# A transformer-like chain in float32 on one core: the shared expert's gate and up products made one product of 128 rows

## What is computed

```python
xn = layernorm(x)
x  = x + attn0(xn) + ffn0(xn)        # layer 0
xn = layernorm(x)
x  = x + attn1(xn) + ffn1(xn)        # layer 1

def ffn0(x):                         # 16 routed experts of 64, top 2, and one shared expert of 64
    shared = (silu(x @ ws_gate) * (x @ ws_up)) @ ws_down
    g = einsum('th,ehm->etm', x, w_gate)
    u = einsum('th,ehm->etm', x, w_up)
    eo = einsum('etm,emh->eth', silu(g) * u, w_down)
    return einsum('te,eth->th', route, eo) + shared
```

## Time and profile before

| what | value |
|---|---|
| median of 3 runs | 2215.48 us (2214.3 to 2218.01) |
| the profiled execution's own time | 2220.59 us |
| its span | 2218.7 us |
| PE busy in the span | 2071.2 us (93%) |
| DVE busy | 1567.6 us (71%) |
| ACT busy | 1207.9 us (54%) |
| POOL busy | 130.4 us (6%) |
| mean granted PE clock | 0.966 |

### The profile page before, as it was taken

One profiled execution on the slowest core, in us unless ns is written; L12 is line 12 of the kernel. 1 busy time (PEld: TensorE's weight loads), 2 busy tenths in 40 slices (PEclk: granted clock), 3 DMA queues, 4 the chain that ended last, 5 costly groups with the idle time before them and its releaser, 6 DMA issues.

```text
span 2218.7 us, 33619 instructions
## 1 busy us (share of the span) xinstructions
PE 2071.2 (93%) x12004; PEld 965.4 (44%) x12088; DVE 1567.6 (71%) x2854; ACT 1207.9 (54%) x2323; POOL 130.4 (6%) x251
## 2 busy tenths in 40 slices
PE   5958999989999999998999999999999999999889
PEld 3621233435656323343656523333565642334356
DVE  5667887756689788673769888775558978877154
ACT  1323677774341667776342367777534156777721
POOL 2000001100000001110000000110000000111000
PEclk9966999999999999999999999999999999999989
DMA  4060100100060010100015010010006001010000
GB/s 154 1 167 5 30 16 26 30 2 1 1 171 6 6 30 23 33 16 2 1 58 119 6 30 15 26 30 3 1 1 157 19 6 30 16 30 17 2 1 10
DMA packets 46983, 71.75 MB, mean 32 GB/s; under 512 B 7968, under 2 KB 17120, under 8 KB 46432
## 3 DMA queue, kind: packets, MB, share of 16 engines
q1 hardware_dynamic: 46816, 69.61, 11.9%
HBM read 46.25 MB, written 22.54 MB: 31 GB/s over the span
## 4 chain that ended last, share of the span: by engine, by line
PE 87%; DVE 5%; ACT 3%; issue 2%; DMA 1%; SPq 0%; POOL 0%; DVEq 0%; ACTq 0%
PE ps L1528 18%; PE ps L1503 16%; PE ps L1472 15%; PE ps L1376 8%; PE ps L1404 8%; PE ps L1396 8%; DVE row_max L1028 3%; PE ps L1538 2%; PE ps L1328 1%; ACT prob L1222 1%; PE ps L1316 1%; PE ps L1297 1%; PE ps L1505 1%; PE ps L1422 1%; PE ps L1322 1%
## 5 line engine op out<-in xcount | busy, mean ns | idle before, releaser
L1222 ACT ACTIVATE prob<-ps 128x512 f32<-128x512 f32 (+3 forms) x1792 | 864.2, 555 | 352.6 <-PE ps L1503 263.6
L1028 DVE TENSOR_REDUCE row_max<-ps 128x1 f32<-128x1024 f32 x512 | 606.1, 1219 | 112.4 <-PE ps L1472 111.7
L1503 PE MATMUL ps<-q_stack,k_stack 96*128 96x512 bf16 (+4 forms) x1760 | 542.6, 362 | 34.4 <-ACT prob L1222 18.7
L1472 PE MATMUL ps<-k_stack,q_stack 96*128 96x512 bf16 (+4 forms) x1740 | 516.6, 368 | 27.6 <-DVE row_max L1028 13.4
L1025 DVE CUSTOM_DVE_ANT_0 tmp<-ps,const_b 128x128 f32<-128x128 f32 (+7 forms) x512 | 371.6, 756 | 131.5 <-PE ps L1472 118.0
L1528 PE MATMUL ps<-prob,v_ones 128*32 128x512 f32 (+3 forms) x3584 | 438.2, 561 | 2.8 <-ACT prob L1222 2.3
L1503 PEld LDWEIGHTS ps<-q_stack,k_stack 96*128 96x128 bf16 (+1 forms) x1792 | 172.2, 98 | 353.6 <-ACT prob L1222 223.7
L1472 PEld LDWEIGHTS ps<-k_stack,q_stack 96*128 96x128 bf16 (+1 forms) x1792 | 149.8, 98 | 383.2 <-issue 100.5
L1376 PEld LDWEIGHTS ps<-wd,prob 128*128 128x128 f32 (+1 forms) x1600 | 206.9, 191 | 69.7 <-issue 62.7
L1165 ACT ACTIVATE prob<-ps 128x512 f32<-128x512 f32 x128 | 76.4, 597 | 272.4 <-PE ps L1396 272.3
L1376 PE MATMUL ps<-wd,prob 128*128 128x128 f32 (+1 forms) x1600 | 212.1, 276 | 1.3 <-DVE prob L933 1.3
(11 more groups left out here) (178 smaller groups left out, 1540.0 us busy)
## 6 DMA issues: line engine op xcount, KB each, us to landing
k_stack<-scratch_k SPq DMA_DIRECT2D x48, 256.0 KB, 6.4
q_stack<-scratch_q SPq DMA_DIRECT2D x48, 256.0 KB, 7.1
scratch_k<-tmp SPq DMA_DIRECT2D x36, 256.0 KB, 2.4
k_stack<-scratch_k SPq DMA_DIRECT2D x96, 64.0 KB, 2.2
q_stack<-scratch_q SPq DMA_DIRECT2D x96, 64.0 KB, 2.2
scratch_k<-tmp SPq DMA_DIRECT2D x36, 128.0 KB, 2.9
scratch_q<-tmp SPq DMA_DIRECT2D x12, 256.0 KB, 2.4
xx<-in_x SPq DMA_DIRECT2D x4, 512.0 KB, 4.2
```

The lines of the kernel that those rows point to most:

```text
L1028: dve.tensor_reduce(nm[G % 2][:, t, j:j + 1], ring_pair(r)[:], AX_X, ALU.max).then_inc(s["ring_used"], 1)
L1222: act.activation(p_slot(v, j)[:, lo - at:hi - at], bank(UNIT_BANKS[u % 3])[:, 0:hi - lo], ACT.Exp, scale=SCALES[kind_of(G)]).then_inc(s["p ...
L1472: ins = pe.matmul(ring_pair(r)[:, lo:hi], queries(G, j)[:, t * P:(t + 1) * P], keys(G, j)[:, lo:hi], start=True, stop=True)
L1503: ins = pe.matmul(dst[:, 0:hi - lo], keys(G, j)[:, kc * P:(kc + 1) * P], queries(G, j)[:, lo:hi], start=True, stop=True)
```

## The change

The weight `ws_up` moves from the end of `wu0` to the end of `wg0`, beside `ws_gate`. The gate product of the shared expert's step then has 128 rows: 64 of gate and, under them, 64 of up, in one bank. The up product of that step is left out, and DVE's second operation reads the up part from partitions 64 to 127 of bank 0. Semaphore counts follow (`UPS` counts the up products), and the gate after a shared step waits for `gu_ready`, since bank 0 is now read by that operation too. In the weave, every gate, of both layers, now also waits for `last(scaled)`, and the shared step's up takes 0.0.

```diff
-                at = do("PE", "gate", 0.88, last(taken), last(ups), xT if n == 0 else None, *(freed if n == 0 else ()))
+                at = do("PE", "gate", 0.88, last(taken), last(scaled), last(ups), xT if n == 0 else None, *(freed if n == 0 else ()))
...
-                ups.append(do("PE", "up", 1.9 if n == 0 else 0.88, at, last(scaled), routed if n == 0 else None, mixed if n == 0 else None))
+                ups.append(do("PE", "up", 0.0 if which == 0 and n % C0 == C0 - 1 else 1.9 if n == 0 else 0.88, at, last(scaled), routed if n == 0 else None, mixed if n == 0 else None))
...
-        wg0 = sb("wg0", (E0 + 1) * M0)
-        wu0 = sb("wu0", (E0 + 1) * M0)
+        wg0 = sb("wg0", (E0 + 2) * M0)
+        wu0 = sb("wu0", E0 * M0)
...
+        def shared(which, n):
+
+            return which == 0 and n % C0 == C0 - 1
...
-                    dve.wait_ge(s["up_psum"], k + 1)
+                    dve.wait_ge(s["up_psum"], UPS[k + 1])
...
-                    dve.scalar_tensor_tensor(gu[k % 2][0:m, :], sg[k % 2][0:m, :], 0.5, bank(U_BANK)[0:m, :], ALU.mult, ALU.mult).then_inc(s["gu_ready"], 1)
+                    ups = bank(G_BANK)[M0:P, :] if shared(which, n) else bank(U_BANK)
+                    dve.scalar_tensor_tensor(gu[k % 2][0:m, :], sg[k % 2][0:m, :], 0.5, ups, ALU.mult, ALU.mult).then_inc(s["gu_ready"], 1)
...
+                if n and shared(which, n - 1):
+                    pe.wait_ge(s["gu_ready"], k)
+                m = P if shared(which, n) else m
                 pe.matmul(bank(G_BANK)[0:m, :], wg[:, c * P:c * P + m], xT[:, tok], start=True, stop=True).then_inc(s["gate_psum"], 1)
...
+                if shared(which, n):
+                    return
```

More of the change, by code:

```diff
@@ L603, in mixture_rows @@
             return M0 if (which, c) == (0, C0 - 1) else P
+        def shared(which, n):
+            return which == 0 and n % C0 == C0 - 1
+        UPS = [0]
+        for what, *how in plan.of("PE"):
+            if what == "gate":
+                UPS.append(UPS[-1] + (not shared(how[1], how[2])))
         def spread_count(b, which, n):
@@ L1338, in front_turn @@
                 if b:
-                    pe.wait_ge(s["up_psum"], plan.step0[b - 1, 0] + 2 * C0)
+                    pe.wait_ge(s["gate_psum"], plan.step0[b - 1, 0] + 2 * C0)
                 for t in range(T):
@@ L1626 @@
         "x": i["L0_attn_encoding"], "R": i["L0_attn_R"], "gate0": i["L0_ffn_gate_w"].T,
-        "wg0": np.concatenate([side(i["L0_ffn_w_gate"]), i["L0_ffn_ws_gate"]], axis=1),
-        "wu0": np.concatenate([side(i["L0_ffn_w_up"]), i["L0_ffn_ws_up"]], axis=1),
+        "wg0": np.concatenate([side(i["L0_ffn_w_gate"]), i["L0_ffn_ws_gate"], i["L0_ffn_ws_up"]], axis=1),
+        "wu0": side(i["L0_ffn_w_up"]),
         "wd0a": rows(i["L0_ffn_w_down"].reshape(-1, D)), "wd0b": i["L0_ffn_ws_down"],
```

## The result

| what | before | after |
|---|---|---|
| median | 2214.89 us (2211.96 to 2218.01) | 2198.11 us (2196.47 to 2200.76, 6 runs) |
| ratio of the two | | 0.9923, 95% interval 0.9913 to 0.9933 |
| profiled execution, its own time | 2220.59 us | 2198.01 us |
| its span | 2218.7 us | 2196.2 us |
| PE / DVE / ACT busy | 2071.2 / 1567.6 / 1207.9 us | 2063.4 / 1559.4 / 1216.3 us |

Faster by 16.8 us, twice the forecast of 8.3. Two of the six runs, 2196.47 and 2196.64 us, lie under the lower edge of the predicted range, 2197; the median lies 1.1 us above it. The traced execution of before was an unusually long one, 5.7 us over its median; the experiments come back to that.

A forecast was written before the change was run, and what follows sets the result against it. PE was taken as the bound, with DVE becoming it among the pieces. 1.7 us in batch 0 plus 2.2 in each of three batches (6.6) made 8.3, so 2207.2 us against the median 2215.48; range 2197 to 2217.

The forecast's parts named there:

- rival A: Hole filled and DVE keeps up: pieces take 55.5 us, each of batches 1 to 3 gains 6.7; 2193.7 us, chance 0.12.
- The product left out: Shared steps: eight up products fewer, two per batch, at 0.86 us each, saving 6.9 us of PE work.
- VectorE's operands: DVE reading up from partitions 64 to 127 of the gate's bank: taken as 0, at worst 5.5 us.
- Batch 0: PE is full there, so two saved products give 1.7 us, down to 0.6 if new waits bite twice.
- Step 1, the hole: PE's 4.3 us idle before q in batches 1 to 3 shrinks to about 2; clock mostly holds, returning 2.6 us.
- Rival B: Clock still falls behind the shorter hole, pieces start at 661.8, each batch gains -0.4 us: 2215.0 us, chance 0.2.
- Step 2, the first piece: Batch 1, xn turn to first piece: 47.6 us under the new order, so it starts at 659.2, ten later.
- Step 3, the pieces: Batch 1's 32 pieces: DVE becomes the bound, 60 us (55.5 to 62.7), last maximum at 719.8, 1.1 us earlier.
- Step 4, the way to the first unit: Batch 1, last piece to turn of the maxima: 6.0 us instead of 7.03, first unit another 1.0 us earlier.
- ACT's table loads and the other queues: Six more 1.28 us loads, 7.7 us on a half-busy ACT, counted in step 1's idle; SP's output queue 0 us.
- Last stretch: Same products in another pattern, PE full before and after: 0, plus or minus 0.5 us.
- the saving is largely spent: Ahead of the xn turn in batch 1, saved products go on DVE's moved work; its second half starts 0.5 us earlier.

The follow-up runs named there:

- E11: The kernel before, unchanged, run and traced once more: 2216.09 us, ratio to before 1.0004.
- E2: The kernel before with only the weave's two lines edited as in the change (new order), both products kept: 2206.67 us, ratio 0.9966.
- E8: E1 plus three unread filler products in front of the turn of xn in batches 1 to 3: 2204.95 us, ratio to before 0.9958.
- E1: The changed kernel with the weave's two lines put back, so merged product in the old order: 2216.33 us, ratio to before 1.0007.
- E3: The kernel before with the shared step's gate and up padded to 128 rows each: 2217.20 us, ratio 1.0007.
- E6: The changed kernel without the gate's added last(scaled) in the weave, the shared up still at 0.0: 2206.56 us, ratio to before 0.9959.
- E7: The kernel before plus three unread filler products in front of the turn of xn in batches 1 to 3: 2213.77 us, ratio 0.9993.
- E10: The changed kernel with the shared step's spread and down widened to 128 rows, plus fillers at five waits of the last closing: 2188.75 us, ratio to before 0.9878.
- E12: E10 plus five fillers before batch 0's turn of xn and 18 products in the wait for the weights: 2185.97 us, ratio to before 0.9870.

## Why the prediction was right, point by point

The direction (faster, under 2211.1 us) and the range of 2197 to 2217 were right, the range narrowly; the size was half, and the forecast's own spread of 2203 to 2211 was missed. Four terms were too small in the same direction: the product, the pieces, the way to the first unit and the last stretch. That the number still fell inside, by 1.1 us, is owed to the room that the range left for rival A, and in part to luck. By the steps of the prediction, against E11's trace:

- **The product left out**, 8 x 0.86 = 6.9 us: mis-sized. It measured 1.13 in the first half of batch 0 and 1.12 to 1.23 in the second, by where one stops reading: 8 x 1.13 to 1.2 = 9.0 to 9.6, and 9.5, good to some 4, between E2 and after. The step took the mean duration of the 64-row form and the start-to-start times of full steps; the timeline of the shared step itself would have shown 0.99, 0.90 and 0.96. The weight loads stayed hidden. The group of line 1404 lost its 16 matmuls of 128*64, as said.
- **VectorE's operands**, taken as 0: right. Line 930 on partitions 64 to 127 took 0.69 us in batch 0 of after at 102.48, line 920 had 0.68. What follows it starts 0.03 us after its end in all eight shared steps, where in seven of before's it overlapped by 0.04 to 0.08: some 0.1 us each at most. The wait behind the shared step: nothing in front of the next gate in the timeline above.
- **Batch 0**, 1.7 us: 2.6 to the turn of `xn` (79.1 to 76.5 us), more by the same mis-sized term; 1.8 of them are left at the first unit (158.4 to 156.6).
- **Step 1, the hole**: under 3 us idle (1.78), clock 1.00, as said. E8 against E1 gives 2.6 us too. Rival B, the clock falling all the same behind a shorter hole, did not come in after. E1 and E3 keep the old hole and say nothing of it, but E6 and E7 in batch 1 show that it was no idle rival: with its waits cut to 1.83, 1.38 and 0.69 us (E6), or to 0.62, 0.30 and 0.69 (E7), q and k still took 5.84 and 5.40 us.
- **Step 2, the first piece**: forecast 659.2 in a batch that starts when it did before. Batch 1's R_w product came 3.2 us early; 655.8 + 3.2 = 659.0. Right.
- **Step 3, the pieces**: "DVE becomes the bound, I take 60". This is the step that was furthest off. Last maximum 712.81 + 1.21 + 3.2 = 717.2, forecast 719.8: from the first piece 58.2 us, forecast 60.6. The sum of 60.8 was right as a sum of durations, but successors overlap by the 0.085 us that the earlier trace rows show all through a stretch without gaps: start to start the maxima are 1.13 us apart from the next operation (711.08 to 712.21), the products 0.60 (712.21 to 712.81). From the end of the first piece it is 57.6, 2.1 over the lower bound of 55.5 and 2.4 under the 60; PE, 57.29 of 57.70 us busy, was as full as DVE.
- **Step 4, the way to the first unit**: 1.0 us shorter forecast, 9.2 instead of 11.3 measured (714.0 to 723.2), 2.2 shorter. The gain also lay elsewhere than forecast: from the last piece to the turn of the maxima it was 6.7 us where 6.0 had been said, and 0.8 came behind that turn (6.2 to 5.4), which the step had left as it was.
- **ACT's table loads and the other queues**, 0: right. ACT has 6 more instructions and is nowhere among PE's releasers in the stretches shown; in after a silu ends at 607.03, a load starts at 607.04, takes 1.28, and the square root starts at 608.34, so nothing stands ahead of the load or behind it; the wait for the maxima's DMA is no longer than before.
- **Last stretch**, 0 +- 0.5: missed: 1.7 us less (90.7 against 92.4 from `wo` to the end of PE's last product), clock for the most part, since `wo` took 3.78 us in before and 2.05 in after.

Per batch 1 to 3, forecast 2.2 us (the steps' own terms, 1.1 and 1.0, give 2.1), measured 6.0 (209.2 to 203.2). Of the 3.8 between, 0.2 lie ahead of the first piece, 2.4 in the pieces and 1.2 behind them. By the experiments the 6.0 are 3.3 of the order (E2: 205.9) and 2.7 of the product. The order's 3.3 are close to the 2.6 of clock, which step 1 had, and the 0.8 behind the turn of the maxima; that is a sum, no run takes them apart. Rival A (2193.7) had the mechanism nearly right, "the hole is filled and DVE keeps up", and lay 4.4 us too low; the truth was between it and the forecast, and nearer to it.

What no part of the prediction saw is that the two gains need each other: 1.7 us in batch 0 and "the saving is largely spent" were argued apart, while E1 shows that in the old order all of the product's gain is given back. That the clock takes it back is shown; why the clock falls where it does is open.

## What to carry to other kernels

When an engine is near full, read three things of a stretch apart: its work at full clock (span times mean clock), where the clock falls, and what is idle in front of each fall. An edit that only removes work may show nothing until the gap that throttles TensorE is gone; measure order and work each alone before dropping either. Filling a gap with idle products can pay (E8, E10), or only move the half clock (E7), so look at the clock again afterwards. Price a narrow product by the starts around it in its own place, not by its duration, and try padding it to the width of its neighbours: here more rows were faster.

## What was not expected of the hardware

- A change between fp32 products of 64 and of 128 output rows cost about 0.1 us each on TensorE: 5.65 us for the shared step's stretch, 5.36 with both products padded to 128 rows; 4.52 with the merged product, 4.26 with spread and down widened as well.
- At the start of the program products take twice their time though the windows give the granted clock as 1.00: in the trace of before 1.91 us for the first up against 1.02 later. Fillers in the wait for the weights removed it (E12). The 1.00 is no measurement: the trace's clock records begin only at 38.4 us in before and 27.4 in E12, and a window counts time without a record as full clock. The row of before, and its window:

```profile
34.07 1.91 PE L1404 MATMUL ps<-xT,wu 128*128 128x512 f32 x2
```

```profile
34.00:39.00 5.00, 5.00 (x15) 2.51 (x14) 1.38 (x2) 1.62 (x2) 0.00 (x0) 1.00 0.00 0
```

- The same instructions in the same order ran with half clock in different places from one execution to the next, worth 3.1 us in one stretch of batch 0 (E11), and kernels that differ elsewhere showed half clock in a stretch that the edit does not touch (E1, E3, E7). For E1 all eleven runs have the low mean clock; E3's runs fall into both kinds (0.963 to 0.966, and 0.968), so there it may be chance.
